# Down product of a gated FFN with adapters: ranks by token half, the 64 left-over features multiplied together with the second adapter factor

## What is computed

```python
def lora_add(base, inp, A, B):
    Ab = A[layer_idx][lora_indices]
    Bb = B[layer_idx][lora_indices]
    t = jnp.einsum('bri,bni->bnr', Ab, inp)
    return base + jnp.einsum('bor,bnr->bno', Bb, t) * SCALE
gate = lora_add(jnp.einsum('bnh,fh->bnf', x, W_gate), x, A_gate, B_gate)
up = lora_add(jnp.einsum('bnh,fh->bnf', x, W_up), x, A_up, B_up)
act = jax.nn.silu(gate) * up
down = lora_add(jnp.einsum('bnf,hf->bnh', act, W_down), act, A_down, B_down)
```

## Time and profile before

| | |
|---|---|
| median of 3 runs | 2098.78 us (2098.72 to 2102.67) |
| span of the profiled execution | 2096.8 us |
| mean granted TensorE clock | 0.984 |
| busy: PE, PEld | 2029.1 us, 1682.9 us |
| busy: DVE, ACT, POOL | 1475.6 us, 744.1 us, 520.8 us |
| DMA | 224.26 MB, mean 107 GB/s |

### The profile page before, as it was taken

One profiled execution on the slowest core, in us unless ns is written; L12 is line 12 of the kernel. 1 busy time (PEld: TensorE's weight loads), 2 busy tenths in 40 slices (PEclk: granted clock), 3 DMA queues, 4 the chain that ended last, 5 costly groups with the idle time before them and its releaser, 6 DMA issues.

```text
span 2096.8 us, 36423 instructions
## 1 busy us (share of the span) xinstructions
PE 2029.1 (97%) x9336; PEld 1682.9 (80%) x9336; DVE 1475.6 (70%) x2422; ACT 744.1 (35%) x1394; POOL 520.8 (25%) x900
## 2 busy tenths in 40 slices
PE   5999899999999999999999999999999999999998
PEld 4777788888887888888888788888888778888886
DVE  3566777777567777777665777777756777777774
ACT  2143333333243333333234333333323443333320
POOL 1232222221142222222123222222113222222200
PEclk8899999999999999999999999999999999999999
DMA  7648444444154655444143655545414564445401
GB/s 199 179 105 156 96 105 106 105 105 98 51 143 96 137 111 111 108 105 100 51 120 87 127 113 111 111 111 111 98 58 124 101 141 111 106 107 111 101 22 41
DMA packets 312832, 224.26 MB, mean 107 GB/s; under 512 B 167992, under 2 KB 302008, under 8 KB 312736
## 3 DMA queue, kind: packets, MB, share of 16 engines
q1 hardware_dynamic: 276256, 194.91, 40.2%
q0 software_dynamic: 35328, 24.03, 6.2%
q10 hardware_dynamic: 1152, 4.19, 0.5%
HBM read 210.18 MB, written 12.58 MB: 106 GB/s over the span
## 4 chain that ended last, share of the span: by engine, by line
PE 78%; issue 8%; POOLq 7%; DVE 3%; ACT 2%; POOL 1%; DMA 1%; DVEq 0%; SPq 0%; ACTq 0%
PE ps L1131 23%; PE ps L1133 22%; PE ps L1132 22%; POOLq L398 6%; PE ps L1294 6%; PE ps L1181 2%; PE ps L1182 2%; DVE ps L748 1%; ACT lora_b L514 1%; PE ps L1157 1%; POOL nat_b L443 1%; PE ps L1155 1%; ACT split L541 0%; DMA nat_b<-L_cond_B_up 0%; DVE acc L888 0%
## 5 line engine op out<-in xcount | busy, mean ns | idle before, releaser
L1131 PE MATMUL ps<-x,split 128*128 128x512 f32 x1440 | 567.2, 394 | 18.3 <-DVE split L734 12.1
L1133 PE MATMUL ps<-x,split 128*128 128x512 f32 x1440 | 563.8, 392 | 0.0
L1132 PE MATMUL ps<-x,split 128*128 128x512 f32 x1440 | 563.3, 391 | 0.0
L541 ACT ACTIVATE split<-ps 128x512 fp32r<-128x512 f32 x368 | 218.9, 600 | 485.6 <-DVE ps L748 473.0
L1131 PEld LDWEIGHTS ps<-x,split 128*128 128x128 f32 x1440 | 272.8, 189 | 74.3 <-issue 13.2
L1133 PEld LDWEIGHTS ps<-x,split 128*128 128x128 f32 x1440 | 272.1, 189 | 59.1
L1132 PEld LDWEIGHTS ps<-x,split 128*128 128x128 f32 x1440 | 272.3, 189 | 57.3
L450 POOL DMA_DIRECT2D nat_ad<-L_cond_A_down x224 | 138.4, 618 | 595.2 <-issue 591.2
L1131 PE MATMUL ps<-hidden 128*128 128x512 f32 (+1 forms) x704 | 275.1, 391 | 6.7 <-DVE acc L942 6.7
L1132 PE MATMUL ps<-hidden 128*128 128x512 f32 (+1 forms) x704 | 274.5, 390 | 0.0
L1133 PE MATMUL ps<-hidden 128*128 128x512 f32 (+1 forms) x704 | 274.3, 390 | 0.0
(11 more groups left out here) (106 smaller groups left out, 2701.7 us busy)
## 6 DMA issues: line engine op xcount, KB each, us to landing
nat<-L_cond_W_gate SPq DMA_DIRECT2D x336, 128.0 KB
nat<-L_cond_W_up SPq DMA_DIRECT2D x336, 128.0 KB
nat_down<-L_cond_W_down SPq DMA_DIRECT2D x112, 384.0 KB
nat<-effective_weight SPq DMA_DIRECT2D x32, 512.0 KB
nat_a<-L_ffn_weight SPq DMA_DIRECT2D x96, 128.0 KB, 2.8
nat<-x SPq DMA_DIRECT2D x16, 512.0 KB
nat_b<-L_cond_B_gate POOLq DMA_DIRECT2D x224, 24.0 KB, 2.1
nat_b<-L_cond_B_up POOLq DMA_DIRECT2D x224, 24.0 KB, 2.1
```

What stands on the lines that cost most here:

```text
L541: act.activation(dst, src, func).then_inc(piece_hi, 1)
L1131: pe.matmul(dst, a[0], b[0], start=first, stop=False)
L1132: pe.matmul(dst, a[0], b[1], start=False, stop=False)
L1133: return pe.matmul(dst, a[1], b[0], start=False, stop=last)
```

## The change

- The pieces DREM move from the head to the end of the last part. The stage `down_rest` of PE is gone, and with it nine `down_add` copies; instead POOL sets `acc` (now ten rows) to zero in each group, in two memsets.
- The ranks of a part are two outputs, one for each half of the tokens. The stationary operand holds the high words of the half's 64 ranks beside their low words, the moving operand the high words of 256 tokens beside their low words: one matmul of 512 columns a tile, 6 instead of 9 in a part. Their four blocks are summed at the end (`down_columns`, `down_ranks`).
- A stage has 10 outputs: two of ranks, eight of W_down. Tile order, banks and DVE's add groups (4, 2, 4 instead of 3, 2, 4) follow. In the last part outputs 3, 4, 5 use banks 0, 1, 2.
- The rest features' activations are kept in `rest_in`, in the 64 rows opposite the ranks of the same token half, and BD and DREM are written to the two halves of two `split` slots. `last_products` then multiplies both at once: for each token half three matmuls of 256 columns and 128 rows. The rest features' ranks are two matmuls more (`ranks_rest`).
- A_down's rest rows are loaded twice (`load_rest`: four DMAs a batch for three).
- `out_sb` moves onto the upper end of `hidden`, hence two new waits for `out_stored`.
- SP: DREM's rows are loaded after D2 of the last part is turned, W_down of part 0 before the sign rows.

```diff
-HEAD = (["B"] * 3 + ["AG"] * 2 + ["AU"] * 2 + ["REM"] * 2 + ["BREM"] + ["DREM"] * 2 + ["ADREM"]
+HEAD = (["B"] * 3 + ["AG"] * 2 + ["AU"] * 2 + ["REM"] * 2 + ["BREM"] + ["ADREM"]
-LAST = PART[:13] + ["BD"] * 2
+LAST = PART[:13] + ["BD"] * 2 + ["DREM"] * 2
...
+            def load_down_rest(g):
+                sp.wait_ge(piece_turned, piece_number(g, NQ - 1, first_of("D2") + 2))
+                for quadrant in range(4):
+                    sp.dma_start(nat_down[32 * quadrant:32 * quadrant + 32, :, 0:32], down_rest[quadrant % 2])\
+                      .then_inc(nat_down_full, 16)
...
-                    pool.dma_start(nat_ad[b % 2:64:2, b // 2, 0:32],
-                                   ad_rest[bass.ds(i, 1)].rearrange("a f r c -> (a f) r c")).then_inc(nat_ad_full, 16)
+                    for half in range(2):
+                        pool.dma_start(nat_ad[64 * half + b % 2:64 * half + 64:2, b // 2, 0:32],
...
                 load_b_down(g)
+                wait(x1_lo, KC * (g + 1))
+                for half in range(2):
+                    pool.memset(acc[:, 5 * half:5 * half + 5, :], 0.0).then_inc(acc_zeroed, 1)
                 wait_turned(g, 0, "ADREM", 1)
...
                 if last:
-                    unit(g, q, "BD", SPLIT_BD - PART_UNITS * q)
+                    for m in (SPLIT_BD, SPLIT_BD + 1):
+                        slot_read(g, q, m - PART_UNITS * q)
+                    last_weights(g, q, "BD", lambda half: half)
                     act_tile(g, q, 2)
+                    last_weights(g, q, "DREM", lambda half: 1 - half)
...
+            def down_columns(g):
+                dve.wait_ge(down_added, ADDED + DOWNS * (g + 1) - KC)
+                dve.wait_ge(act_lo, START + ACTS * (g + 1))
+                dve.tensor_tensor(act_f[:].rearrange("p (h t) -> p h t", h=2), acc[:, KC:, 0:256], acc[:, KC:, 256:512],
+                                  ALU.add).then_inc(ranks_added, 1)
...
-                    b_down_unit(g, q, SPLIT_BD)
+                    b_down_unit(g, q)
                     act_tile(g, q, 2)
-                    down_add(g, q + 1, 0)
-                    rank(g, 2)
-                    for i in range(1, 9):
-                        down_add(g, q + 1, i)
-                        if i == 5:
+                    down_rest(g, q)
+                    for i in range(2):
+                        down_add(g, q, i, LAST_BANKS)
+                    down_columns(g)
+                    last_lows(g, q, "DREM", lambda half: 1 - half)
+                    down_ranks(g)
+                    for i in range(2, STAGE):
+                        down_add(g, q, i, LAST_BANKS)
+                        if i == 6:
                             down_low(g, 0)
...
-                for i in range(3):
-                    down_add(g, q + 1, i)
+                for i in range(4):
+                    down_add(g, q, i)
...
+                def ranks(half, js, stop):
+                    tokens = HALVES[half][1]
+                    for j in js:
+                        mm = pe.matmul(ps[:, banks[half], :].rearrange("p (s t) -> p s t", s=2),
+                                       lora_ad[:, j, 2 * half:2 * half + 2, :].rearrange("p b r -> p (b r)"),
+                                       acts[:, :, j, tokens], start=(j == 0), stop=(stop and j == PT - 1))
+                    return mm
...
+                def last_products(i):
+                    for half, (_, tokens) in enumerate(HALVES):
+                        mm = product(ps[:, banks[i], tokens], stationary(SPLIT_BD + half, i - 2),
+                                     [rest_in[:, s, tokens] for s in range(2)], False, half == 1)
+                    mm.then_inc(down_psum, 1)
...
                 def bank_read(i):
-                    pe.wait_ge(down_added, DOWNS * g + 9 * (q + 1) + i - 2)
+                    pe.wait_ge(down_added, ADDED + DOWNS * g + STAGE * q + max(0, i - 2))
...
-                for i in range(3):
-                    bank_read(i)
-                    tiles(i, (0, 1))
+                bank_read(0)
+                for half in range(2):
+                    ranks(half, (0, 1), False)
+                tiles(2, (0, 1))
                 pe.wait_ge(act_lo, START + ACTS * g + PT * q + 4)
                 if not last:
-                    for i in range(3):
-                        tiles(i, (2,)).then_inc(down_psum, 1)
-                    for i in range(3, 9):
+                    for half in range(2):
+                        ranks(half, (2,), True).then_inc(down_psum, 1)
+                    tiles(2, (2,)).then_inc(down_psum, 1)
+                    for i in range(3, STAGE):
                         bank_read(i)
                         tiles(i, range(PT)).then_inc(down_psum, 1)
                     return
...
+                for half in range(2):
+                    ranks(half, (2,), False)
+                    ranks_rest(half).then_inc(down_psum, 1)
+                tiles(2, (2,), False)
+                pe.wait_ge(up_read, START + ACTS * (g + 1))
+                for i in (3, 4, 5):
+                    tiles(i, range(PT), False)
                 pe.wait_ge(piece_lo, START + LOW_PIECES * (g + 1))
                 pe.wait_ge(rank_lo, START + 3 * g + 3)
-                for i in (1, 2, 3):
-                    adapter(i)
-                for i in range(4, 9):
+                for i in (2, 3, 4, 5):
+                    last_products(i)
+                for i in range(6, STAGE):
                     bank_read(i)
                     tiles(i, range(PT), False)
-                    adapter(i)
+                    last_products(i)
```

More of the change, by code:

```diff
@@ L595, in rank, with down_ranks @@
                 act.wait_ge(rank_sum, 3 * g + n + 1)
[L596 to L601, removed]
+                for rows, tokens in HALVES:
+                    copy(lora_t[rows, n, 1, tokens], act_f[rows, tokens])
+                copy(lora_t[:, n, 0, :], act_f[:]).then_inc(rank_hi, 1)
+            def down_ranks(g):
+                act.wait_ge(ranks_added, g + 1)
+                for (rows, tokens), (other, _) in zip(HALVES, HALVES[::-1]):
+                    last = copy(gated[rows, tokens], act_f[other, tokens])
+                last.then_inc(ranks_moved, 1)
+                act.wait_ge(rank_sum, 3 * g + 3)
+                for rows, tokens in HALVES:
+                    last = copy(rest_in[rows, 0, tokens], act_f[rows, tokens])
+                last.then_inc(rank_hi, 1)
             def act_rest(g):
@@ L617, in act_tile, with last_weights @@
                 copy(acts[:, 0, j, :], act_f[:]).then_inc(act_hi, 1)
+            def last_weights(g, q, name, slot_of):
+                c = first_of(name)
+                for half in range(2):
+                    cols = slice(512 * half, 512 * half + 512)
+                    act.wait_ge(piece_turned, piece_number(g, q, c + half) + 1)
+                    for i, (rows, _) in enumerate(HALVES):
+                        last = copy(split[rows, slot_of(i), 0, cols], bank_of(c + half)[rows])
+                    last.then_inc(piece_hi, 1)
             def part(g, q, last):
@@ L840, in a_down_rest @@
-                piece_low(g, 0, c, lora_ad[0:64, 1, 0, :], bank_of(c)[0:64, 0:P], lora_ad[0:64, 0, 0, :])
+                dve.wait_ge(nat_ad_full, 128 * (9 * g + 2))
+                turn(g, 0, c, bank_of(c)[:, 0:P].rearrange("p (b a) -> p b a", b=4), nat_ad[:, :, 0:32])
+                dve.wait_ge(piece_hi, piece_number(g, 0, c) + 1)
+                for i, ((_, _), (other, _)) in enumerate(zip(HALVES, HALVES[::-1])):
+                    last = lo(ad_rest[other, 1 - i, :], bank_of(c)[other, 64 * i:64 * i + 64], ad_rest[other, i, :])
@@ L1086, in group @@
                 act_rest(g)
[L1087 to L1088 removed]
+                dve.wait_ge(acc_zeroed, 2 * g + 2)
+                dve.wait_ge(out_stored[0], 64 * (START + g))
                 sign_unit(g, 0)
@@ L1251, in tiles, with ranks_rest @@
+                def ranks_rest(half):
+                    rows, tokens = HALVES[1 - half][0], HALVES[half][1]
+                    return pe.matmul(ps[:, banks[half], :].rearrange("p (s t) -> p s t", s=2),
+                                     ad_rest[rows].rearrange("p b r -> p (b r)"), rest_in[rows, :, tokens],
+                                     start=False, stop=True)
                 def tiles(i, js, stop=True):
-                    m = DOWN_ORDER[i]
                     for j in js:
-                        w = [(down_w[:, s, j, m, :] if m < KC else lora_ad[:, s, j, :]) for s in range(2)]
-                        mm = product(ps[:, D_BANK + i % 3, :], w, [acts[:, s, j, :] for s in range(2)],
-                                     j == 0, stop and j == PT - 1)
```

197 lines of the change are left out of this document (104 added, 93 removed).

## The result

| | before | after | a second profile of after |
|---|---|---|---|
| median of the runs | 2100.58 us | 2183.67 us (2174.53 to 2187.62) | 2176.45 us (2174.67 to 2180.07) |
| span of the profiled execution | 2096.8 us | 2184.5 us | 2173.9 us |
| mean granted clock | 0.984 | 0.966 | 0.969 |
| PE's waits on an `acc` add | 6.7 us | 75.5 us | 75.8 us |

The ratio to the kernel before is 1.0387 (95% interval 1.0364 to 1.0409). In a second comparison on one chip with other kernels it is 1.0376 (1.0360 to 1.0392). The prediction was 2174.7 us, range 2140 to 2203.

What follows compares the result with a forecast made beforehand. Taken to bound the changed kernel: PE's waits for DVE's `acc` adds and POOL's load queue. Terms of 25.1, 8.2, 26.6, 10.0 and 6.0 us added 75.9 to the 2096.8 us span; with 2.0 for the median, 2174.7, range 2140 to 2203.

Runs made afterwards that it cites:

- (1): The changed kernel with five PSUM banks instead of three for the down outputs, in all parts but the last: 2114.26 us.

## What to carry to other kernels

Count how many matmuls stand between a bank's last write and its reuse: shrinking work ahead of a hand-over moves the wait and saves nothing, while more banks cost nothing where they are free (1). In a queue of loads ask first which ones the next deadline needs; moving one load that is due much later gained more here (44.7 us) than either way of shortening the queue (24 to 34). And a step that is moved takes its wait along: look up which event its number means in the new place.

## What I had not expected of the hardware

A batch's load on POOL is mostly the reading of its table value: a gap of about 1.8 us, 1.5 of it two dependent reads on the sequencer, for 0.6 us of each DMA issue, and the sequencer reads on while POOL works: a pair of memsets of 4.4 us was free, a second pair cost its 4.6. PE's clock fell after waits of 1.76 to 1.80 us in 2 to 6 of 15 stages and after none of the 1.68 us ones, at 1.6 us each; after waits of 7 to 14 us it fell every time. Matmuls that alternate between stationary operands of 128 and 64 rows start 0.43 us apart, not 0.227.
